# Split operands, large transfers and the order of a down projection in a fused attention, MLP and adapter kernel

## The reference, cut to what matters

```
q, k, v = x @ Wq, x @ Wk, x @ Wv
a   = softmax(q k^T * 512**-0.5) v @ Wp + bp
cms = gelu(a @ cW1 + cb1) @ cW2 + cb2 + one_hot(code)      # 512 -> 2048 -> 512
mod = gelu([a, cms] @ mW1 + mb1) @ mW2 + mb2               # 1024 -> 2048 -> 512
y0  = clip(x + cms + mod, 0, 1)
for each of 3 layers:                                      # weights W[expert of the sequence]
    h = gelu(y @ W_down + b_down) @ W_up + b_up            # 512 -> 256 -> 512
    y = layernorm(y + h) * gamma + beta
```

## Time and profile before

| what | value |
|---|---|
| median of 3 runs | 1243.22 us (1242.97 to 1245.54) |
| the profiled execution: its own time | 1244.26 us |
| the profiled execution: its span | 1242.3 us |
| granted clock of TensorE, mean | 0.992 |
| PE busy | 1193.2 us, 96% |
| DVE busy | 786.3 us, 63% |
| ACT busy | 558.5 us, 45% |
| POOL busy | 346.1 us, 28% |
| 16 DMA engines, mean rate | 111 GB/s |

### The profile page before, as it was taken

The page is one execution under the profiler, slowest core; times in us unless marked ns, Lnnn a source line. Parts: engine busy times, 40 slices in busy tenths (PEclk is TensorE's granted clock), DMA queues, the critical chain, the costliest instruction groups (busy, mean ns, idle before and its releaser), DMA issues.

```text
span 1242.3 us, 15219 instructions
## 1 busy us (share of the span) xinstructions
PE 1193.2 (96%) x5312; PEld 977.0 (79%) x5312; DVE 786.3 (63%) x1271; ACT 558.5 (45%) x1056; POOL 346.1 (28%) x347
## 2 busy tenths in 40 slices
PE   7999989998999999999999999999999999899887
PEld 5888868776888788888877888878888888788776
DVE  5444385684766855564657766585555654779986
ACT  5334353543433635252524433454343344366666
POOL 1332222201210213040411220122222222588871
PEclk9999999998999999999999999999999999899999
DMA  5765442143110202020383111111111116645544
GB/s 188 261 214 175 163 158 96 52 200 121 52 51 17 90 12 94 10 95 7 104 337 119 51 58 45 35 51 52 51 51 51 51 43 213 236 155 185 170 145 160
DMA packets 50625, 137.42 MB, mean 111 GB/s; under 512 B 6372, under 2 KB 6372, under 8 KB 46838
## 3 DMA queue, kind: packets, MB, share of 16 engines
q1 hardware_dynamic: 50550, 136.46, 31.8%
HBM read 103.92 MB, written 32.52 MB: 110 GB/s over the span
## 4 chain that ended last, share of the span: by engine, by line
PE 74%; POOL 9%; DVE 8%; ACT 4%; issue 3%; DMA 2%; SPq 1%; POOLq 0%; DVEq 0%; ACTq 0%
PE psum L508 73%; POOL res L1435 3%; POOL res L1437 3%; DMA wraw<-dn_w_dram 1%; POOL yT L1416 1%; ACT z L958 1%; POOL sm L1428 1%; DVE ring L1126 1%; DVE g_hl L1164 1%; DVE w_t L1138 1%; SPq L420 1%; DMA wq_raw<-wts_dram 1%; DVE w_hl L1157 0%; DVE v_t L1132 0%; DVE g L1144 0%
## 5 line engine op out<-in xcount | busy, mean ns | idle before, releaser
L508 PE MATMUL psum<-g_hl,w_hl 128*128 128x512 f32 x1536 | 352.8, 390 | 0.9 <-DVE g L1152 0.9
L508 PE MATMUL psum<-a_ops,ring 128*128 128x512 f32 x1344 | 322.8, 393 | 15.9 <-DVE w_t L1138 9.2
L508 PEld LDWEIGHTS psum<-g_hl,w_hl 128*128 128x128 f32 x1536 | 287.9, 188 | 63.4 <-DVE g L1152 3.6
L508 PEld LDWEIGHTS psum<-a_ops,ring 128*128 128x128 f32 x1344 | 252.7, 189 | 74.7 <-DVE w_t L1138 11.8
L1402 POOL TENSOR_TENSOR asum<-rawp 128x256 f32<-128x256 f32 x48 | 36.1, 752 | 654.3 <-DVE ring L1126 628.9
L1164 DVE TENSOR_TENSOR g_hl<-g,g_hl 128x512 fp32r<-128x512 f32 x128 | 95.9, 753 | 114.6 <-ACT g_hl L872 113.8
L508 PE MATMUL psum<-c_ops,ring 128*128 128x512 f32 x672 | 163.9, 390 | 0.5 <-DVE c_ops L1207 0.5
L508 PEld LDWEIGHTS psum<-c_ops,ring 128*128 128x128 f32 x672 | 125.7, 188 | 28.3 <-DVE c_ops L1207 2.4
L1126 DVE TENSOR_TENSOR ring<-asum,ring 128x256 fp32r<-128x256 f32 x192 | 95.4, 498 | 68.7 <-ACT ring L832 68.7
L832 ACT CAST ring<-asum 128x256 fp32r<-128x256 f32 x192 | 77.0, 404 | 125.1 <-PE psum L508 124.4
L872 ACT CAST g_hl<-g 128x512 fp32r<-128x512 f32 x128 | 78.6, 618 | 106.5 <-PE psum L508 106.5
(11 more groups left out here) (120 smaller groups left out, 1472.1 us busy)
## 6 DMA issues: line engine op xcount, KB each, us to landing
rawp<-up_w_dram SPq DMA_DIRECT2D x48, 512.0 KB, 3.5
wdu_split<-prep SPq DMA_DIRECT2D x36, 512.0 KB, 2.9
wraw<-dn_w_dram SPq DMA_DIRECT2D x64, 256.0 KB, 2.8
wd<-wdu_split SPq DMA_DIRECT2D x12, 1024.0 KB, 7.5
wu<-wdu_split SPq DMA_DIRECT2D x12, 1024.0 KB, 5.5
prep<-wdu_dram SPq DMA_DIRECT2D x36, 256.0 KB, 3.3
second_pair_operands<-c_ops SPq DMA_DIRECT2D x7, 1024.0 KB, 11.4
a_ops<-second_pair_operands SPq DMA_DIRECT2D x7, 1024.0 KB, 11.5
```

Source lines behind the costliest of these rows:

```text
L508: ins = nc.tensor.matmul(ps, lw(el), rw(er), start=first and i == 0, stop=last and i == 2, skip_group_check=skip)
```

## The change

- **Down projection by sequence.** Operand d is now sequence d // 4 with weight tile d % 4. All four split tiles are kept (`w_hl` has four buffers), each raw tile lies in the half of its buffer that its lo part will take, and the four weight splits stand in the second quad of the up steps, ahead of the first gelu tiles. Split gelu tiles have two buffers. The banks of the first sequence are added at the fifth operand.
- **SP's wait for a raw down weight tile** is now for PE's last use of its buffer in the chunk before. Its place in the list is the same.
- **Order inside a quad of the second MLP.** Part 1 goes P1, P7, P5, P6; V and W stand at step 8 (before: 6 and 7).
- **Operands of the first pair.** Three are split behind the value tiles of sequence 2, the sums and the others behind the attention rows.
- **Operands of the second pair.** P1 and P2 are split in sequence 3's value product, the four sums are made by POOL, the rest in chunk 0. The seven stores stand behind the fourth weight tile of chunks 1, 2 and 3, the loads one by one in chunk 7, four of them ahead of its fourth weight tile.
- **y0.** The first pair's y0 is made in the buffer `xs[0]` in chunk 8, split in chunks 9 and 10, stored split, and loaded as `yT` in chunk 15 ahead of its fourth weight tile. The x of the second pair is added in the last down projection.

```diff
-               tuple((i, e) for e in range(2) for i in range(4)) + tuple((i, e) for i in range(4, PROD) for e in range(2)))
+               tuple((i, 0) for i in (P1, P6, P7, P5)) + tuple((i, 1) for i in (P1, P7, P5, P6))
+               + tuple((i, e) for i in (P2, P4, P3) for e in range(2)))
-GHL = 3
+GHL = 2
...
-        w_hl = [at(f"w_hl{i}", 120 + 4 * i, [P, 2, V], F32R) for i in range(2)]
+        w_hl = [at(f"w_hl{i}", k, [P, 2, V], F32R) for i, k in enumerate((172, 120, 124, 152))]
+        wraw = [at(f"wraw{i}", k + 2, [P, V]) for i, k in enumerate((172, 120, 124, 152))]
...
-        U_AT, V_AT, W_AT, C22_AT, C21_AT = (1, 5), (2, 6), (3, 7), (4, 8), (6, 12)
-        G12_AT, G22_AT, G11_AT, G21_AT = (1, 1), (5, 9), (5, 10), (6, 13)
-        PRE_AT = ((2, 3, 4, 5, 6), (4, 6, 8, 10, 12))
+        U_AT, V_AT, W_AT, C22_AT, C21_AT = (1, 5), (2, 8), (3, 8), (4, 9), (6, 12)
+        G12_AT, G22_AT, G11_AT, G21_AT = (1, 1), (5, 10), (5, 11), (6, 13)
+        PRE_AT = ((1, 2, 3, 4, 5, 6), (2, 4, 6, 8, 10, 12))
...
             def down_weights(t):
-                if t >= 2:
-                    sp.wait_ge(w_lo_done, t - 1)
-                sp.dma_start(wraw[t % 2][:, :], dn_w[t % (2 * HT)]).then_inc(s_wraw[t % 2], 16)
+                if t < 4:
+                    sp.wait_ge(bank_full, J_PV3 + DT)
+                else:
+                    sp.wait_ge(d_used, 32 * (t // 4 - 1) + 16 + 4 * (t % 4) + 4)
+                sp.dma_start(wraw[t % 4][:, :], dn_w[t % (2 * HT)]).then_inc(s_wraw[t % 4], 16)
...
                 down_weights(4 * ci + 2)
+                if ci == NCHUNK - 1:
+                    for i in (P1, P6, P7, P5):
+                        next_a_operand(ci, i)
+                if ci == NCH - 1:
+                    for b in range(2):
+                        sp.wait_ge(aop_used, aop_at(ci, 1) + 2 + 2 * b)
+                        sp.dma_start(f(yT[b][:, :, :, :]), y0_split[b]).then_inc(s_yTin[b], 16)
                 down_weights(4 * ci + 3)
...
             def down_chunk(ci):
                 for d in range(DSTEP):
-                    k, q = divmod(d, 2)
+                    q, k = divmod(d, 4)
...
-                            if at_ in (0, 3):
-                                down_weight_hi(ci, at_ // 3)
+                            if at_ < 4:
+                                down_weight_hi(ci, at_)
                             else:
-                                g_hi(ci, {1: 0, 2: 1, 4: 2}[at_])
+                                g_hi(ci, at_ - 4)
```

More of the change, by code:

```diff
@@ L140, in build @@
         rawp = [at(f"rawp{i}", 160 + 4 * i, [P, 4, 2 * P]) for i in range(NRAW)]
-        wraw = [at(f"wraw{i}", 172 + 2 * i, [P, V]) for i in range(2)]
         ring = [at(f"ring{i}", 192 + 2 * i, [P, 2, 2 * P], F32R) for i in range(RING)]
-        xs = [at(f"xs{i}", k, [P, 2, DT, S]) for i, k in enumerate((56, 48))]
+        xs = [at(f"xs{i}", k, [P, 2, DT, S]) for i, k in enumerate((56, 32))]
+        y0_hl = at("y0_hl", 72, [P, 2, 2, DT, S], F32R)
         yT = [at(f"yT{b}", 16 * b, [P, 2, DT, S], F32R) for b in range(B)]
@@ L247, in build @@
         gelu_done = sem("gelu_done")
-        s_wraw = [sem(f"down_weights_landed_raw_{i}") for i in range(2)]
+        s_wraw = [sem(f"down_weights_landed_raw_{i}") for i in range(4)]
         w_hi_done = sem("down_weight_hi_done")
@@ L259, in build @@
         s_y0in = [sem(f"y0_landed_{i}") for i in range(2)]
+        y0_hi_done = sem("first_pair_y0_hi_done")
+        y0_lo_done = sem("first_pair_y0_lo_done")
+        s_y0split = sem("first_pair_y0_split_stored")
+        s_yTin = [sem(f"y0_split_landed_{i}") for i in range(2)]
+        x_added = sem("x_of_second_pair_added")
         t_wd = [sem(f"down_weights_landed_{i}") for i in range(2)]
@@ L795, in piece, with after_v @@
                         piece_hi(b + 1, c + m)
-                def first_pair_rows(m):
-                    if b == 2 and m < 3:
+                def after_v(m):
+                    piece(0, m)
+                    if b == 2:
                         if m == 0:
@@ L801, in first_pair_rows, with after_u @@
                         attention_hi(0, (P1, P3, P2)[m])
-                    elif b == 2:
-                        attention_hi(0, P7, after_sum=1)
-                hi_jobs(n + JV, LOW, lambda m: v_n[:, 0, m, :], after=lambda m: piece(0, m), tiles=(0, 1, 2))
-                hi_jobs(n + JPT, HIGH, lambda m: pT[:, 0, m, :], after=first_pair_rows)
+                def after_u(m):
+                    piece(2 * PSLOT, m)
+                    if b == 2 and m == 0:
+                        attention_hi(0, P4, after_sum=4, after_lo=PROD - 1)
+                hi_jobs(n + JV, LOW, lambda m: v_n[:, 0, m, :], after=after_v, tiles=(0, 1, 2))
+                hi_jobs(n + JPT, HIGH, lambda m: pT[:, 0, m, :])
                 hi_jobs(n + JV + DT, LOW, lambda m: v_n[:, 0, m, :], tiles=(3,))
-                if b == 2:
-                    attention_hi(0, P5, after_sum=2)
                 x_hi_parts(b + 1)
@@ L859, in down_weight_hi @@
                 t = 4 * ci + k
-                act.wait_ge(s_wraw[t % 2], 16 * (t // 2 + 1))
-                if t >= 2:
-                    act.wait_ge(d_used, 4 * (2 * (t - 2) + 2))
-                nc.scalar.copy(w_hl[t % 2][:, 0, :], wraw[t % 2][:, :]).then_inc(w_hi_done, 1)
+                act.wait_ge(s_wraw[k], 16 * (ci + 1))
+                nc.scalar.copy(w_hl[k][:, 0, :], wraw[k][:, :]).then_inc(w_hi_done, 1)
             def g_hi(ci, d):
                 t = DSTEP * ci + d
-                k, seq = divmod(d, 2)
+                seq, k = divmod(d, 4)
                 q, row = divmod(k, 2)
@@ L996, in _ @@
                     z_norm(9)
[L997 to L998 removed]
+                if s == 0:
+                    y0_hi(3)
                 if 2 <= s:
@@ L1218, in _, with second_pair_y0 @@
+            def second_pair_y0(seq):
+                for m in range(DT):
+                    dve.wait_ge(d_evac, 8 * (NCH - 1) + 4 * seq + m + 1)
+                    nc.vector.tensor_scalar(res[:, 2 + seq, m, :], res[:, 2 + seq, m, :], 0.0, 1.0, ALU.max, ALU.min).then_inc(y0_done, 1)
             for n in range(AHEAD):
@@ L1411, in _ @@
                 weight_sums(n)
-            for b in range(B):
+                if n in (1, 2):
+                    second_pair_sums(n - 1)
+                if n in (PPIECE + 4, PPIECE + 5):
+                    first_pair_y0_lo(n - PPIECE - 4)
+            for b in range(2, B):
                 for d in range(DT):
-                    pool.wait_ge(t_y0hi, b * DT + d + 1)
+                    pool.wait_ge(t_y0hi, (b - 2) * DT + d + 1)
                     nc.gpsimd.tensor_tensor(yT[b][:, 1, d, :], res[:, b, d, :], f(yT[b][:, 0, d, :]), ALU.subtract).then_inc(t_y0lo, 1)
```

300 lines of the change are left out of this document (167 added, 133 removed).

## The result

The changed kernel takes **1305.68 us** (median of four runs, 1304.08 to 1314.38), the kernel before 1243.41 beside it (1242.97 to 1245.54). The ratio is 1.0511, with a 95% interval of 1.047 to 1.0551: slower by about 5%. The forecast was 1302 with a range of 1262 to 1322. The profiled execution took 1305.86, with a span of 1304.1, which is 61.8 more than the span before; the sum had said +58.6.

A forecast was written before the change was run, and what follows sets the result against it. The prediction took PE, busy 96% and carrying 74% of the chain, as the bound. Terms -6.2 - 3.9 + 15.2 + 6 + 38.8 + 13 + 2 - 6.3 gave +58.6 on the median 1243.22: 1302 us, range 1262 to 1322.

The forecast's parts named there:

- What bounds the kernel: Whole program: PE is busy 96% and carries 74% of the chain, so what the change inserts is lost in full.
- Second-layer chunks: Chunks 4, 5, 6, 12, 13, 14: third down weight tile lands late, delaying W, plus slow clock; +38.8 us, the largest term.
- Chunk 7: Four 1 MB operand loads ahead of the fourth weight tile make PE start 10.8 late at C22; with the clock +13 us.
- Chunk 15: Two 2 MB loads stand ahead of the fourth weight tile, which lands near T 35; +2 us.
- Attention: Third sequence's attention: DVE pieces for first-pair operands no longer stand ahead of the last value tile; -6.2 us.
- chunk 1: Seven 1 MB stores issued together delay pieces and weights; spreading them leaves an ordinary first-layer loss of 3.1; -3.9 us.
- tail: After the last down projection: first-pair split loaded from DRAM and additions made earlier, so POOL's scaling starts sooner; -6.3 us.
- First-layer chunks: Chunks 2, 3, 8 to 11: extra weight tiles delay W, C22 and the down projection; +2.3 each, +15.2 us with y0 work.
- plus 1.4 for the y0 work of the first pair in chunks 8 to 10: Part of the first-layer +15.2: first-pair y0 work in chunks 8 to 10 costs 1.4 us.
- Chunk 0: POOL takes four 1024-wide sums and DVE pieces beside them slow down; +6 us, the middle of 0 and +12.
- Faster: Rival: tile in SBUF by T 29.5, W on time, DVE keeping up in the first layer; 1225 us, chance 0.07.
- The waits do not reach PE: Rival: ACT and DVE waits are absorbed, second layer costs nothing; +10, 1253 us; partial absorption, 1246 to 1262, chance 0.06.

The follow-up runs named there:

- Experiment 1: Changed kernel with SP issuing all four down weight tiles of a chunk together, ahead of ring pieces, chunk 7's operand loads and chunk 15's loads: 1252.65 us.
- Experiment 2: Changed kernel with only chunk 7's fourth down weight tile issued ahead of the four operand loads: 1305.17 us in a single execution.
- experiment 5: Kernel before, with three first-pair operands made behind the third sequence's value tiles and the sums behind its attention rows: 1237.13 us.
- experiment 6: Kernel before, with the seven 1 MB stores spread behind the weights of chunks 1, 2 and 3 instead of together in chunk 0: 1237.48 us.
- experiment 3: Changed kernel with POOL's 1024-wide sums of chunk 0 and y0 pieces of chunk 9 each cut into four: 1307.32 us in a single execution.
- experiment 8: Changed kernel with tiles issued first, first-layer g operands earlier and weight tiles later, narrow POOL y0 pieces, y0 work in down parts of chunks 8 and 9: 1237.52 us.
- experiment 4: Changed kernel with both g operands made earlier and two weight tiles later in first-layer chunks: 1306.13 us in a single execution.
- 9: Kernel of experiment 8 with C12's addition and gelu moved behind the third g operand in first-layer chunks: 1225.67 us.

## Why the prediction was right, and where it was off

**What bounds the kernel: right.** "Whatever the change inserts there is lost in full" held: the six second-layer chunks had no slack, and PE's gaps came back one for one in the time.

**Second-layer chunks: right in mechanism, and in size with some luck.** The step was 4.6 of waiting and 1.7 of clock per chunk; chunk 5 shows 4.48 and 1.57, all six +39.6 for +38.8. But the 4.6 were made up otherwise: W was to be 3.8 late and the down projection 0.8 more, and in chunk 5 W alone is 4.48 late and the down projection runs without a further gap. I took the landing as 4.5 between bounds of 2.4 and 4.8; in the rows of chunk 5 it is 5.3 from SP's issue to ACT's copy, outside the bounds, and ACT waits 6.2 for it where 4 to 5 were forecast. And over all six the late starts at W sum to 26.0 where 28.6 of waiting were forecast, and the rest, clock but for 0.6, to 13.7 where it was 10.2. The two errors cancel. The estimate from the fit in the Trainium skill (DMA: Bandwidth & Descriptors, Anatomy of one DMA), which gave 3.5 for this landing and a sum 6 lower, does not agree with the trace, so the nearest row was the better choice, though it was short too. Experiment 1 shows the cause.

**Chunk 7: right**, +14.8 for +13: PE's step that waits for C22 starts 12.0 late for 10.8 forecast, and the clock makes the rest. Experiment 2 splits it: 7.5 for the tile behind the operand loads, the rest as in any chunk of this layer. **Chunk 15: right**, +2.0; with the tiles first it goes too.

**Attention, chunk 1, tail: right**, -6.6, -4.2 and -6.6 for -6.2, -3.9 and -6.3. The first was also measured alone at -6.5 (experiment 5), the spread stores at -6.15 in a kernel whose first-layer chunks have not the changed order (experiment 6). The tail was not isolated; the same 180.7 to 181.7 us from the last down product to the end in every kernel with that code, against 186.3 to 187.3 in every kernel without, speak for it.

**First-layer chunks: the step that failed** is "plus 1.4 for the y0 work of the first pair in chunks 8 to 10". It measured 9.0: chunk 9 alone lost 9.9, of which 2.0 are the ordinary loss, and chunk 8 1.1 beyond it. I gave no reason for its size and no row; in fact DVE waits out 2.6 us pieces of POOL (experiment 3), in front of W and of the down projection, where it has no slack. Chunk 8's 1.1 was not taken apart: experiment 8 moved its y0 work and changed the order too. The ordinary +2.3 was +2.03: the up steps lost 1.0 for 1.4 forecast, the start of the down projection 1.56 for 1.5. I had the late start of the down projection from the tiles ahead of the g operands (experiment 4 confirms it), but did not see that C12's gelu stands behind that, and would take its place as soon as the start is on time (experiments 8 and 9).

**Chunk 0: off**, +3.2 for +6. The right reason for taking more than the 1.22 stood in the text: DVE pieces do wait for wide POOL ones here too (a ring piece of 0.42 takes 2.02 at 218.37 in the changed kernel). That the six DVE pieces less paid for more of it than I gave them is likely, but no run shows it. Which of the two, the longest block or POOL's total, sets the remaining 2 to 3 us in chunk 0 stays open: narrow pieces made it worse by 1.7 in one execution, and a kernel with these sums elsewhere was not tried.

These errors, +7.6 for y0, -2.8 for chunk 0, -1.6 for the six ordinary losses, +1.8 in chunk 7 and -1.7 for a start that was chance, partly cancel, so the total of 1302 was nearer to 1305.7 than its terms deserved.

**The rivals.** "Faster" had the right place: the point at which the third tile is in SBUF decides. But its 1225 needed DVE to keep up in the first layer as well, and experiment 1, which moves only that point, ends at 1252.65. "The waits do not reach PE" had 1253, and experiment 1 ends there, but not by its mechanism: the waits did reach PE wherever the tile was late. Without the late tile the change costs 10 us net, by first-layer order and POOL; that this equals the rival's sum, which had far less for y0 and more for chunk 0, is partly luck.

## What to carry to other kernels

An operand that becomes needed earlier must also be *issued* earlier: read the transfer queue's order, not only the engine's, and put what the next instruction wants ahead of what is prefetched for later (here one reordered queue was worth 53 us). On an in-order engine look at each wait for what is queued behind it: V and W behind a weight tile, the third operand behind a gelu that the seventh needs. And read the effect of an edit by stretches; two single executions here showed no gain in total while the edited stretch gained 7.5 and 4 to 6 us.
